# Attention scores from stacked fp16 parts, exponentials on keys by queries, and a pass over three steps

## The reference, cut to what matters

```python
hs      = mha(x @ Wq, ctx[:124] @ Wk, ctx[:124] @ Wv)        # FIRST, 8 heads
ca_hs1  = mha(ca_q1, x, x)                                   # CA, 8 heads, ca_q1 = ca.T[indices] @ Wq_ca
ca_hs2  = mha(ca_hs1 @ Wq, ca @ Wk_ca, ca @ Wv_ca)           # 4 keys
x = (hs + ca_hs2) @ Wout + b_out + x
h = ln(x);  x = attn(h, h, q1, k1, v1) @ o1_w + o1_b + x     # SELF, 20 heads
h = ln(x);  x = attn(h, ctx, q2, k2, v2) @ o2_w + o2_b + x   # CROSS, 20 heads
a, g = split(ln(x) @ ff_w1 + ff_b1)
out = a * gelu(g) @ ff_w2 + ff_b2 + x
```

## Time and profile before

| | |
|---|---|
| median of 3 runs | 4387.28 us (4378.07 to 4389.27) |
| the profiled execution | 4387.02 us, its span 4385.2 us |
| mean granted TensorE clock | 0.983 of full speed |
| instructions | 98793 |

### The profile page before, as it was taken

One profiled execution on the slowest core, in us unless ns is written; L12 is line 12 of the kernel. 1 busy time (PEld: TensorE's weight loads), 2 busy tenths in 40 slices (PEclk: granted clock), 3 DMA queues, 4 the chain that ended last, 5 costly groups with the idle time before them and its releaser, 6 DMA issues.

```text
span 4385.2 us, 98793 instructions
## 1 busy us (share of the span) xinstructions
PE 4089.1 (93%) x32700; PEld 2973.8 (68%) x32700; DVE 2826.6 (64%) x6624; ACT 2214.3 (50%) x6060; POOL 1412.0 (32%) x1681
## 2 busy tenths in 40 slices
PE   5999999999999999999999999999999999999999
PEld 4666667666667666666666666666666666676666
DVE  6666666666666666666666666666666666666665
ACT  1454555454555454555454555554554545554544
POOL 0333333333333333333233333233333232333332
PEclk9999999999999999999999999999999999999999
DMA  3000000000000000000000000000000000000000
GB/s 119 9 2 13 13 13 12 11 4 13 13 13 12 11 4 13 13 13 12 11 4 13 13 13 12 10 5 13 13 13 12 5 10 13 13 12 13 2 13 15
DMA packets 46226, 58.78 MB, mean 13 GB/s; under 512 B 5449, under 2 KB 45073, under 8 KB 45201
## 3 DMA queue, kind: packets, MB, share of 16 engines
q1 hardware_dynamic: 45585, 50.89, 3.7%
HBM read 40.39 MB, written 10.49 MB: 12 GB/s over the span
## 4 chain that ended last, share of the span: by engine, by line
issue 39%; PE 34%; POOL 15%; DVE 5%; ACT 5%; POOLq 0%; DMA 0%; DVEq 0%; SPq 0%; ACTq 0%
PE bank L1037 32%; POOL KM L395 9%; ACT P L540 3%; DVE nmax L755 2%; PE bank L1158 1%; POOL rstd L418 1%; DVE PT L766 1%; POOL VX L412 1%; PE bank L1082 1%; POOL VX L411 1%; POOL xrest L410 1%; ACT PT L532 1%; POOL X L382 1%; ACT V L499 1%; POOL rstd L417 1%
## 5 line engine op out<-in xcount | busy, mean ns | idle before, releaser
L540 ACT ACTIVATE P<-bank,nmax 128x128 f32<-128x128 f32 (+1 forms) x3584 | 1033.4, 382 | 344.1 <-DVE nmax L755 341.9
L766 DVE SCALAR_TENSOR_TENSOR PT<-bank,PT 128x512 f16<-128x512 f32 (+4 forms) x1024 | 635.8, 621 | 299.6 <-ACT PT L532 295.7
L755 DVE TENSOR_REDUCE nmax<-bank 128x4 f32<-128x512 f32 (+4 forms) x1024 | 633.0, 618 | 274.9 <-PE bank L1037 267.4
L1158 PEld LDWEIGHTS bank<-ident,P 128*128 128x128 f32 (+1 forms) x3584 | 437.8, 142 | 460.1 <-issue 258.8
L532 ACT ACTIVATE PT<-bank 128x512 f16<-128x512 f32 (+4 forms) x1024 | 569.3, 556 | 287.5 <-PE bank L1158 272.1
L417 POOL TENSOR_TENSOR rstd<-mv,eps 128x1 f32<-128x1 f32 x192 | 40.2, 210 | 2013.0 <-DVE mv L790 2013.0
L1158 PE MATMUL bank<-ident,P 128*128 128x128 f32 (+1 forms) x3584 | 582.6, 279 | 48.7 <-ACT P L540 48.7
L1037 PE MATMUL bank<-hT,w_ff_w 128*128 128x256 f16 x5280 | 623.5, 273 | 1.3 <-DVE hT L716 1.3
L1037 PEld LDWEIGHTS bank<-hT,w_ff_w 128*128 128x128 f16 x5280 | 509.7, 98 | 74.1 <-issue 14.0
L1037 PE MATMUL bank<-KM,QB 128*128 128x512 f32 (+3 forms) x1024 | 488.5, 580 | 46.3 <-ACT QA L487 26.9
L1037 PE MATMUL bank<-KM,QA 128*128 128x512 f32 (+3 forms) x1024 | 491.4, 572 | 0.0
(11 more groups left out here) (207 smaller groups left out, 5762.7 us busy)
## 6 DMA issues: line engine op xcount, KB each, us to landing
xin<-in_x SPq DMA_DIRECT2D x33, 320.0 KB
out<-X SPq DMA_DIRECT2D x64, 160.0 KB, 1.8
xT<-in_xT SPq DMA_DIRECT2D x66, 120.0 KB
cT<-in_cT SPq DMA_DIRECT2D x66, 96.0 KB
raw_ff_w<-in_ff_w SPq DMA_DIRECT2D x1, 3840.0 KB, 15.7
xT<-in_xT SPq DMA_DIRECT2D x33, 80.0 KB
w_ff<-in_ff_w SPq DMA_DIRECT2D x1, 1600.0 KB
raw_q<-in_q SPq DMA_DIRECT2D x2, 480.0 KB, 5.4
```

The costliest lines, as they stand in the source:

```text
L540: last = nc.scalar.activation(P[:, x % 3, h * keys:(h + 1) * keys], s_bank[x % 3][:, h * keys:(h + 1) * keys], ACT.Exp, bias=nmax[:, x % 3 ...
L755: nc.vector.tensor_reduce(nmax[:, x % 3, 0:m], s_bank[x % 3][:, 0:m * keys].rearrange("p (h s) -> p h s", h=m), axis=AX.X, op=ALU.max, neg ...
L766: nc.vector.scalar_tensor_tensor(out=PT[0:keys, n % 2, 1, 0:m * S], in0=bank[0:keys, 0:m * S], scalar=P_SCALE, in1=PT[0:keys, n % 2, 0, 0: ...
L1158: last = nc.tensor.transpose(bank[0:keys, h * S:(h + 1) * S], P[:, n % 3, h * keys:(h + 1) * keys], ident[:, :])
```

## The change

**Scores.** Queries and keys become two fp16 parts each (`cQ`, `cK`: a high part by ACT; the low one by DVE, or, for K1, Q1 and Q2, by POOL's `low_split` from a whole fp32 copy made by DVE). SP stores both parts to scratch in DRAM (`put`, 18 DMAs a step) and loads them back by head (`stack`, 18 DMAs a step), so that one head's contraction holds three products of parts, stacked on partitions: query parts (high, high, low) on key parts (high, low, high), 48 rows for heads of 16, 120 for heads of 40. CA's queries are not made; `token_gains` multiplies `x` by the token weights instead, and POOL's `token_queries` places the tokens by head.

**Exponentials.** A unit is four heads everywhere, 28 units a step. Per unit: four fp16 matmuls of 128 columns for scores on queries by keys (`scores`), whose maxima DVE takes; for each group (attention and sequence, 8 in a step) one fp32 transpose of the maxima and two small copies to fp16 parts; then `exponents` computes the scores again on keys by queries and adds the negated maxima with a second matmul (`pick`), 8 fp16 matmuls of 128 columns. ACT takes the exponential of 512 columns twice, to fp32 (`P`) and to fp16 (`PT`), and POOL subtracts them (`low_probabilities`). The `P` transposes, ACT's copy and DVE's subtraction are gone, and so are `mask_keys` and `KM`.

**Order.** All eight PSUM banks are now six job banks and two output banks. A pass handles SELF and CROSS of one step, CA and FIRST of the next, and the feed-forward of the one before; the loop makes 33 passes, and the last feed-forward stays in the tail. The order is written out in each engine's block; `BODY` below shows PE's, with S for `scores`, T for `exponents` and mx for `turn_maxima`. SP's queue holds, per pass, 18 stores to scratch, 18 loads from it, 9 input loads (the context now twice) and two output stores.

```diff
-J_BANKS = 4
+J_BANKS = 6
...
-ALL_UNITS = [(att, b, u) for att in range(4) for b in range(G) for u in range(len(ATT_UNITS[att]))]
+QK_EXP = 11
+Q_PARTS = (0, 0, 1)
+K_PARTS = (0, 1, 0)
+ROWS_D0, ROWS_D1, ROWS_CA = 3 * D0, 96, 96
+MAX_EXP = 14
+MAX_LOW = 64
+MAX_ROWS = MAX_LOW + HEADS1
...
+CA, SELF, CROSS, FIRST = range(4)
+ATT_UNITS = (2, 5, 5, 2)
+KEYS = (S, S, S, KEYS0)
+GROUPS = [(att, b) for att in range(4) for b in range(G)]
+ALL_UNITS = [(att, b, u) for att, b in GROUPS for u in range(ATT_UNITS[att])]
 UNITS_STEP = len(ALL_UNITS)
-STREAMS = ((0, 12), (12, 22), (22, 32))
...
+P_SLOTS, PT_SLOTS = 2, 3
...
+BODY = jobs_of("""
+    XT0_0 XT0_1 K1T0 K1T1 K1T2 Q1T0 Q1T1 Q1T2
+    S0 S1 V1_0 mx0 S2 S3 V1_1 T0 mx1 T1 kca T2 vca T3 M4 Q0T0
+    S4 S5 Q0T1 S6 S7 Q0T2 S8 caT0 caT1 mx2 S9 S10 K0T0
+    T4 S11 K0T1 T5 S12 K0T2 T6 S13 s4 T7 mx3 V0_0 T8 V0_1 T9 T10 T11 outT1_0 T12 T13 outM1_0
+    ff0 ff1 outT1_1 ff2 outM1_1 ff3 p4T ff4 XT1_0 XT1_1 ff5 Q2T0 Q2T1 Q2T2 mT ff6 mB ff7 ff8 ff9
+    S14 S15 y0 S16 S17 S18 K2T0 mx4 S19 S20 K2T1
+    T14 S21 T15 S22 T16 S23 T17 mx5 T18 T19 S24 T20 S25 T21 outT2_0 mx6 S26 T22 S27 T23 outM2_0
+    T24 mx7 T25 T26 outT2_1 T27 V2_0 outM2_1 hs0 V2_1 outT0_0 K2T2 hs1 outM0_0 outT0_1 outM0_1 y1
+    XT2_0 XT2_1 G
+""")
...
+            def put(src, k, r, dst, at, landed):
+                sp.dma_start(dst[:, at:at + r, :].rearrange("a p n -> p a n"), src[0:r, :, k, :]).then_inc(landed, 16)
+            def stack(dst, src, e, parts, landed):
+                for y, part in enumerate(parts):
+                    sp.dma_start(dst[y * e:(y + 1) * e, :, :],
+                                 src[part, :, :].rearrange("(h e) n -> e h n", e=e)).then_inc(landed, 16)
...
+            def one_pass(i, stores):
+                put_splits(i, "K1T", cK, s_k1, self_put)
+                put_splits(i, "Q1T", cQ, s_q1, self_put)
+                sp.wait_ge(j_full, done(i - 1, LOOP_JOBS.number("T23"), "J"))
+                sp.wait_ge(self_put, i * STACK_STORES + STACK_STORES)
+                stack(Ks, s_k1, D1, K_PARTS, self_stacked)
+                stack(Qs, s_q1, D1, Q_PARTS, self_stacked)
+                put_lows(i, "Q0T", cQ, CH0, s_q0, AT0, first_put, self_stacked)
+                put_lows(i, "K0T", cK, CH0, s_k0, AT0, first_put)
+                sp.wait_ge(j_full, done(i - 1, LOOP_JOBS.number("T27"), "J"))
+                sp.wait_ge(first_put, i * STACK_STORES + STACK_STORES)
+                stack(Q0s, s_q0, D0, Q_PARTS, first_stacked)
+                stack(K0s, s_k0, D0, K_PARTS, first_stacked)
+                sp.wait_ge(v_done, v_job(i, LOOP_JOBS, "V0_1"))
+                sp.wait_ge(xa_ready, i * G + G)
+                sp.wait_ge(ca_ready, i + 1)
+                sp.wait_ge(vx_ready, i * G + G)
+                load_step(i + 1, i)
+                sp.wait_ge(k2_put, i * CROSS_STORES + CROSS_STORES)
+                sp.wait_ge(j_full, done(i, LOOP_JOBS.number("T13"), "J"))
+                stack(Ks, s_k2, D1, K_PARTS, cross_stacked)
+                put_splits(i, "Q2T", cQ, s_q2, q2_put, first_stacked)
+                sp.wait_ge(q2_put, i * CROSS_STORES + 2 * CROSS_STORES)
+                stack(Qs, s_q2, D1, Q_PARTS, cross_stacked)
+                if stores:
+                    put_out(i, 0)
+                put_lows(i, "K2T", cK, CH1, s_k2, AT1, k2_put, cross_stacked)
+                if stores:
+                    put_out(i, 1)
...
-            def mask_keys(i, att, b, src, rows, heads, mask):
...
+            def low_probabilities(i, n):
+                att, b, u = ALL_UNITS[n]
                 keys = KEYS[att]
+                pool.wait_ge(a_done, done(i, LOOP_JOBS.number(f"T{n}", "A"), "A"))
+                nc.gpsimd.tensor_tensor(PT[0:keys, n % PT_SLOTS, 1, :], P[0:keys, n % P_SLOTS, :],
+                                        PT[0:keys, n % PT_SLOTS, 0, :], ALU.subtract).then_inc(low_p, 1)
...
+            def low_split(i, name, k, dst):
+                r, m = CH1[k], SPLITS[name] + k
+                pool.wait_ge(v_done, v_job(i, LOOP_JOBS, f"{name}{k}"))
+                nc.gpsimd.tensor_tensor(dst[0:r, 1, k, :], whole[0:r, m % 3, :], dst[0:r, 0, k, :], ALU.subtract)\
+                    .then_inc(split_done, 1)
...
+            def token_queries(i):
+                link(i, nc.gpsimd.tensor_tensor(ca32[:, :], ca32[:, :],
+                                                next_factor[0:rows, FCA:FCA + 1].to_broadcast([rows, GS]), ALU.mult))
+                link(i, nc.gpsimd.tensor_tensor(ca16[:, :], ca32[:, :],
+                                                one_col[0:rows, 0:1].to_broadcast([rows, GS]), ALU.mult))
+                link(i, nc.gpsimd.tensor_tensor(ca16[low, :], ca32[low, :], ca16[low, :], ALU.subtract))
+                nc.gpsimd.tensor_tensor(ca_heads[:, :, :], ca16[:, :].unsqueeze(1).to_broadcast([rows, HEADS0, GS]),
+                                        mask_ca[:, :].unsqueeze(2).to_broadcast([rows, HEADS0, GS]), ALU.mult)\
+                    .then_inc(ca_ready, 1)
...
-            def stream(i, first, end, pre, post):
...
-                            last = nc.scalar.activation(
-                                P[:, x % 3, h * keys:(h + 1) * keys], s_bank[x % 3][:, h * keys:(h + 1) * keys],
-                                ACT.Exp, bias=nmax[:, x % 3, h:h + 1])
-                        last.then_inc(s_exp, 1)
+            def exps(i, n):
+                bank = bank_of(i, LOOP_JOBS, f"T{n}")
+                if n >= PT_SLOTS:
+                    act.wait_ge(pv_done, units_done(i, n - PT_SLOTS))
+                else:
+                    act.wait_ge(pv_done, units_done(i - 1, UNITS_STEP - 1))
+                act.wait_ge(low_p, units_done(i, n - P_SLOTS))
+                if n == LAST_UNIT[SELF, 1] + 1:
+                    act.wait_ge(v_done, v_job(i, LOOP_JOBS, f"ff{FFT - 1}"))
+                nc.scalar.activation(P[0:keys, n % P_SLOTS, :], bank[0:keys, :], ACT.Exp, bias=log_p[0:keys, :], scale=by)
+                nc.scalar.activation(PT[0:keys, n % PT_SLOTS, 0, :], bank[0:keys, :], ACT.Exp, bias=log_p[0:keys, :],
+                                     scale=by).then_inc(a_done, 1)
...
+            def maxima(i, n):
+                bank = bank_of(i, LOOP_JOBS, f"S{n}")
+                nc.vector.tensor_reduce(mx[:, g % 2, 4 * u:4 * u + 4],
+                                        bank[:, :].rearrange("p (h s) -> p h s", h=4)[:, :, 0:keys],
+                                        axis=AX.X, op=ALU.max, negate=True).then_inc(v_done, 1)
...
-            def queries_ca(i, jobs):
-                for c, r in enumerate(CH0):
-                    mm(j_next(i, jobs, "q1ca", c)[0:r, 0:GS], w_qca[:, AT0[c]:AT0[c] + r], caG[:, :])\
-                        .then_inc(j_full, 1)
...
+            def token_gains(i, jobs):
+                bank = j_next(i, jobs, "G")
+                pe.wait_ge(step_loaded, i * LOADS_STEP + 2 * LOADS_STEP)
+                for k, rk in enumerate(CH0):
+                    last = mm(bank[0:ROWS_CA, 0:GS], w_ca[0:rk, k, :], xT[0:rk, k, :], k == 0, k == 2)
+                last.then_inc(j_full, 1)
...
-            def stream(i, first, end, pre, mid, post, queries):
...
+            def operands(att, b, head):
+                s = slice(b * S, (b + 1) * S)
+                if att == CA:
+                    return ca_heads[:, head, s], G16[:, s]
+                if att == FIRST:
+                    return Q0s[:, head, s], K0s[:, head, b * S:b * S + KEYS0]
+                return Qs[:, head, s], Ks[:, head, s]
+            def scores(i, n):
+                if (b, u) == (0, 0):
+                    if att == CA:
+                        pe.wait_ge(ca_ready, i + 1)
+                        v_job_done(i - 1, LOOP_JOBS, "G")
+                    else:
+                        pe.wait_ge({SELF: self_stacked, CROSS: cross_stacked, FIRST: first_stacked}[att],
+                                   i * STACK_LOADS + STACK_LOADS)
+                bank = j_next(i, LOOP_JOBS, f"S{n}")
+                for h in range(4):
+                    q, k = operands(att, b, 4 * u + h)
+                    last = mm(bank[:, h * S:h * S + keys], q, k)
+                last.then_inc(j_full, 1)
+            def turn_maxima(i, g):
+                att, b = GROUPS[g]
+                heads = HEADS0 if att in (CA, FIRST) else HEADS1
+                bank = j_next(i, LOOP_JOBS, f"mx{g}")
+                v_job_done(i, LOOP_JOBS, f"S{LAST_UNIT[att, b]}")
+                nc.tensor.transpose(bank[0:heads, 0:S], mx[:, g % 2, 0:heads], ident[:, :]).then_inc(j_full, 1)
+            def exponents(i, n):
+                if u == 0:
+                    v_job_done(i, LOOP_JOBS, f"mx{g}")
+                for h in range(4):
+                    q, k = operands(att, b, 4 * u + h)
+                    o = bank[0:keys, h * S:(h + 1) * S]
+                    mm(o, k, q, True, False)
```

(29 more changed lines are left out.)

1494 lines of the change are left out of this document (839 added, 655 removed).

## The result

The changed kernel takes 4523.61 us, median of four runs (4515.12 to 4531.92), beside 4385.99 for the kernel before in the same series: a ratio of 1.0316, 95% interval 1.0292 to 1.0340. The forecast was 4015, with a range up to 4270 and 0.12 for slower. Both the sign and the size were wrong.

The account below looks back on a forecast made before the run. PE's issue was taken as the bound: 132.35 us a pass less 19.3 (PE work) less 6.2 (old losses) plus 10.0 (new waits) made 116.9; 33 passes plus head and tail gave 4015 us, range 3790 to 4270.

Parts of the forecast that it names:

- PE's work: TensorE's matmuls and transposes in a pass: 47.4 us before, 28.1 after, so 19.3 us saved.
- The rule of the Trainium skill: fp16 128-column matmuls on TensorE: about 81 ns each in a sustained stream, about 8.7 us more PE work a pass.
- The other engines: Per unit: ACT's pair 1.23 us (bounds 0.60 to 1.4), POOL's subtraction 1.08 (0.78 to 1.38); no engine but PE full.
- Head and tail: Time outside the repeated passes: 150 us before, plus 6 for the change.
- The new waits: PE waiting in T14 to T27, the pass end, SELF's units and starts of groups: together 10.0 us a pass.
- T14 to T27: CROSS exponents units and those after: ACT has 19.1 us, PE 13.5, so 5.6 us of waiting.
- the end of a pass: After the last unit, up to the next K1: DVE's chain 14.5 us against PE's 12.3, costed at 2.5 us.
- rival 3: New pauses in SELF and CROSS units halve TensorE's clock: 5.5 us, 122.4 a pass, 4197 us; chance 0.12.
- the sign named for it: In the trace, long stretches of clock 0.5 behind PE's pauses would show the forecast wrong.
- let these 6.2 us go: CA and FIRST stretch: 4.0 us idle, plus 2.2 us a step of half-clocked work, both counted as gone.
- Cost at nothing, covered by PE's other work: POOL's 28 subtractions a pass, 1.08 us each, put at no cost; uncovered unit chain ACT 1.23, POOL 1.08, PE 0.31.
- Rival 4: Scratch stores and loads before S4 and S14 come 12 to 15 us late: 130 a pass, 4450 us; chance 0.12.

Follow-up runs that it names:

- e5_fill_all: The changed kernel plus 252 spare fp16 matmuls a pass, 6 ahead of each unit's low-part wait and 84 in the pause at the pass head: 4558.20 us, ratio 1.0396.
- e9_short_chain: The changed kernel with one exponential a unit instead of two, and GpSimd subtracting only 128 of 512 columns of each low part: 4172.08 us, ratio 0.9513.

## Why the prediction was wrong, by its own steps

- **PE's work: nearly right.** A 128-column fp16 matmul takes 0.058 us in a stream, where 0.055 was taken; a scores unit has 0.22 and an exponents unit 0.46 between starts (forecast 0.22 and 0.44). The rule of the Trainium skill (TensorE: Matmul & The Clock Gate, section Back-to-back issue gap), some 81 ns, does not show here: the stream has 58 ns at full clock. Taking the clock's 10.9 us off PE's busy time leaves 105.3 us a pass where 103.2 was forecast. The price of the matmul explains 336 x 0.003 = 1.0 of the 2.1.
- **The other engines: nearly right one by one.** ScalarE's pair is 1.34 us instead of 1.23, GpSimd's subtraction 1.155 instead of 1.08, inside the bounds given. Head and tail were 146 instead of 156.
- **The new waits: nearly right in sum, by luck.** Idle time is 2.9 us above the forecast, but stands elsewhere: from T14 to T27 it is 3.9 us where 5.6 was put down, and from T27 to the next T0 it is 6.8 where 2.5 stood for the end of a pass. The pause at the head alone took 5.6: the terms summed busy times of VectorE and had no row for its turn of the loop body (2.35 us).
- **The clock: the step that failed.** The forecast's sum put nothing down for half-clocked work. The text saw that the changed units would make PE wait in T14 to T27, and priced this at 5.6 us of waiting; what the clock does to the work beside such waits stood only in rival 3, at 5.5 us a pass and a chance of 0.12. It measured some 11, the largest part of the 15.8, and the sign named for it, long stretches of clock 0.5 behind the pauses, is what the trace shows. The size came from 45 us at a clock of 0.84, the worst stretch of before; the stretches here have 0.54 and 0.55, and not only in the SELF and CROSS units: the head of the pass, the tail of CA's units and the token products have it too. And "let these 6.2 us go" took the 2.2 us of old half clock as saved, with no run for it.
- **Where it was lost.** From T14 to T27 the forecast had 19.1 us, set by ScalarE, and 22.0 were measured. Of the 2.9 the dearer pair makes 14 x 0.11 = 1.5; e5_fill_all, at full clock there, still takes 20.5, so the clock makes about 1.5. Most of the half-clocked work there lies in time that ScalarE takes anyway. The other 12.9 us are missing outside T14 to T27 (110.7 against 97.8): 13.6 us of work at 1.2 GHz, worth an estimated 6.2, 4.6 of idle time, 2.1 of dearer work.
- **A chain was costed as a cover.** "Cost at nothing, covered by PE's other work" was put against GpSimd. In the units PE has 0.99 us of work and GpSimd 1.16 and ScalarE 1.34; three quarters of the subtraction alone are worth 3.0 us a pass, and with the exponential 10.8. Not all of the 10.8 is part of the miss: e9_short_chain also takes away waiting that the forecast had counted (16.2 us from T14 to T27 where it had 19.1), so the chain stands for at most 7.9 of the 15.8 us.
- **Rival 4: near in size (4450), wrong in mechanism.** PE waits 7.3 us in the whole run for the stacks. But the hop has no more slack than forecast (1.8 us): three loads more ahead of each set brought 4.4 us of waiting.

What is left open: e9_short_chain stays 5.0 us above 116.9. Its idle time equals the forecast's in sum only (13.8 against 13.65; 6.8 of it from T27 to T0). Its busy time is 108.1 against 103.2; 5.1 us of it are at 1.2 GHz, worth 2.3, and the matmuls' price makes 1.0, so 1.6 were not traced. Why CA's units lose the clock in some kernels and not in others is not shown: their time at 1.2 GHz goes from 0.3 to 11.6 us, and in e5_fill_all it was 10.6 with their waits filled.
